# Query projections as products of high and low parts, and work handed between VectorE and GpSimd

## The chip, the cores and the metric

The kernel runs on one core of one Trainium2 chip. The metric is the device time of one execution in microseconds (us), taken as the median of the runs. The chip's engines are TensorE (PE; its weight loads are listed as PEld), VectorE (DVE), ScalarE (ACT), GpSimd (POOL) and SyncE (SP), which issues most of the DMAs. Each has its own queue of instructions and waits for the others on semaphores. SBUF is the memory on the core, PSUM holds the results of TensorE in eight banks of 128 x 512 float32.

## What is computed

The reference, cut to what matters. x has 2 x 1024 tokens of 256 features, the context 2 x 77 rows.

```python
def xattn(q, kv, Wq, Wkv, Wc):                     # q is layernorm(x), kv the context
    qp = jnp.einsum('bld,ed->ble', q, Wq)
    scores = jnp.einsum('bld,bmd->blm', qp, kv)
    idx = jnp.argmax(scores, axis=-1)              # one context row for each token
    mem = jnp.take_along_axis(kv, idx[..., None], axis=1)
    mk, mv = jnp.split(jnp.einsum('bld,ed->ble', mem, Wkv), 2, axis=-1)
    qh = qp.reshape(b, l, 16, 16).transpose(0, 2, 1, 3)
    attn = softmax(jnp.einsum('bhlm...') * 0.25)   # 16 heads, one key and value head
    out = jnp.einsum('bhlm,bmd->bhld', attn, mv)
    return jnp.einsum('bld,ed->ble', out, Wc)

def ffn(x, w1, w2, router_w):                      # 8 experts of 512, 2 for each token
    probs = softmax(x @ router_w.T)
    topk_w, sel = top_k(probs, 2)
    ...                                            # silu(gate) * up, then w2, weighted sum

x = x + xattn(layernorm(x), ctx, Wq, Wkv, Wc)
x = x + ffn(layernorm(x), w1, w2, router_w)
```

Every product must come out nearly as exact as float32, since the choices (argmax, top 2) hang on it.

## The kernel before, in words

**Stages.** 2048 tokens are 16 tiles of 128 (T), taken in NH = 4 chunks of HT = 4 tiles, 512 tokens each (QW). A first stage does, per chunk u, the moments of the layernorm (VectorE), 1/sqrt of the variance as a power (`rs`, GpSimd) and -mean/sqrt (`nm`, GpSimd), the normalised rows `xn` (`x_normal`, ScalarE), their transposition on TensorE (`turn_x`, line 1306 of the kernel) and the copy of it out of PSUM as `xT` (`turned`, ScalarE, line 607; the trace calls it pT, since it lies in that buffer's space). From `xT` come the scores against the context (`score`, line 1319), which use W_q folded into the context beforehand, and the projection to queries (`project`, line 1332).

**The projection.** `project(u, j)` computes 128 of the 256 query features of a chunk: two float32 matmuls of 128 rows by 512 columns. ScalarE rounds the result to fp32r (`q_high`, line 612) and VectorE subtracts that from PSUM to get the rest (`q_low`, line 810); fp32r is a float32 format of fewer bits, which TensorE takes in one pass. High and low parts lie in `qhl`. The later products all use such pairs: high times high, low times high, high times low.

**Picks.** `picks(u)` on VectorE (lines 786 to 806) finds each token's best context row: `sd` (line 791), four `max`, four `max_index`, the scores for the router `x0` (line 800), a cast of the index to float (line 802) and four comparisons with a constant `iota_n` that give one-hot rows `oh` (line 805). `counts(b)` on TensorE sums these for a batch of two chunks, and `picked`, `replaced` and `spread` on VectorE make from it the masked keys `kb` and values `vc` (line 847) of that batch. `logits(u, k)` on TensorE (line 1365) multiplies queries and keys, and `maxima(u, k)` on VectorE (line 861) takes the largest per head. When the eight of chunk 0 are there, they are turned and cast (`maxima_turned`, `mT`, line 616), and the attention proper begins: `scores_turned`, `exps` (line 623), `sums`, `normalise`, `combine`, `residual`, then the router's choice and the placing of tokens into blocks (`choose`, `scaled`, `slots`, `columns`, `hots`, `table`, lines 904 to 990).

**The experts.** From about 140 us on 39 blocks of 128 places are gathered, multiplied with the weights of their expert (`inner`, line 1633, `outer`, line 1642) and added into the output, in a fixed round of TensorE, ScalarE, VectorE and GpSimd.

**The weights' low parts.** The experts' weights (48 pieces of 128 x 512) are loaded as float32 into `raw`. `W` lies over `raw`, two pieces lower. ScalarE's `high` (line 602) rounds a piece to fp32r into `W`, GpSimd's `splits` (line 502) subtracts in two halves of 256 columns and writes the low part as bf16 into a ring of LR = 3 buffers, and SP's `keep_lows` (line 389) stores it to memory, to be read back later. `high` of piece n waits for the low part n - 2, `splits` of piece n >= 3 for the store of n - 3. How many pieces ScalarE takes at which point of its queue is a table, `HIGH_HEAD` for the first stage (seven pieces) and `HIGH_SLOT` for the attention; `exps` stands in the same queue.

**Order.** There is no scheduler: each engine's queue is the order in which its function is written (`@block.tensor` and so on, at the end of each). In the first stage TensorE goes: turns(0), score(0), turns(1), score(1), project(0), router product, counts(0), project(1), turns(2), score(2), project(2), turns(3), logits(0, 0), half of score(3), logits(0, 1), the other half, logits(0, 2), project(3, 0), logits(0, 3), project(3, 1), the other logits. VectorE goes: moments of all chunks, some clearing (lines 1006 to 1013), picks(0), picks(1), q_lows(0), the masks of batch 0, q_lows(1), picks(2), q_lows(2), then maxima with picks(3) and the last q_low between them.

**Buffers with nine elements.** `slot`, `sloti`, `bki`, `rmi` and `rmf` hold 8 numbers and a spare one; `odd()` gives them as 3 x 3.

## Time and profile before

| what | value |
|---|---|
| median of 3 runs | 353.85 us (352.81 to 359.24) |
| the profiled execution | 353.84 us |
| its span, first to last instruction | 352.0 us |
| TensorE, weight loads | 323.9 us (92%), 221.7 us (63%) |
| VectorE, ScalarE, GpSimd | 192.2 (55%), 211.8 (60%), 193.1 us (55%) |
| mean granted clock of TensorE | 0.986 of full speed |
| moved by DMA | 43.77 MB, 124 GB/s |

The profile is of one execution, and its span leaves out 1.84 us around the instructions. A busy time is the sum of the instructions of an engine; TensorE's matmuls are pipelined, so it can be called busy in a stretch in which it isn't at its peak. A float32 matmul is recorded as two. A number behind "x" is a count, L with a number the line of the kernel.

### The profile page before, as it was taken

The numbers are of one execution on the slowest core, as the hardware profiler recorded it, in microseconds if no ns is written. First come the engines' busy times: TensorE is split into PE (matmuls) and PEld (weight loads), VectorE is DVE, ScalarE is ACT, GpSimd is POOL, SyncE is SP. The second block draws the span as 40 slices with busy tenths as digits, with TensorE's granted clock in tenths as the row PEclk, the third lists the DMA queues.
The fourth block names the chain that finished last, engine by engine and source line by source line (L and its number), as shares of the span: only waits on it lengthen the run. The fifth ranks groups of instructions, "written<-read, shape, count | busy, mean of one in ns | idle before, by whom it ended". The sixth has DMA issues, their size and how long they took to land.

```text
span 352.0 us, 7569 instructions
## 1 busy us (share of the span) xinstructions
PE 323.9 (92%) x2324; PEld 221.7 (63%) x2325; DVE 192.2 (55%) x648; ACT 211.8 (60%) x380; POOL 193.1 (55%) x215
## 2 busy tenths in 40 slices
PE   7998989998988899999999999999999999999940
PEld 3855544454444545786767777777777777777730
DVE  3996865636769799787884333333333333333310
ACT  1927427876788693856655556666556665566620
POOL 3401637876868783656766555545555554555330
PEclk9999999999999999999999999999999999999995
DMA  8999535825254377925234432333332333333221
GB/s 239 373 386 387 189 108 163 242 78 181 76 164 151 124 226 242 299 64 153 47 92 64 73 63 49 59 52 53 61 59 34 58 61 61 61 48 51 39 30 15
DMA packets 35690, 43.77 MB, mean 124 GB/s; under 512 B 3312, under 2 KB 28272, under 8 KB 35664
## 3 DMA queue, kind: packets, MB, share of 16 engines
q1 hardware_dynamic: 27088, 32.58, 27.9%
q0 software_dynamic: 7488, 10.39, 18.3%
q10 hardware_dynamic: 1088, 0.46, 0.6%
q8 instruction: 15, 0.25, 0.3%
q14 instruction: 11, 0.09, 0.1%
HBM read 27.49 MB, written 15.93 MB: 123 GB/s over the span
## 4 chain that ended last, share of the span: by engine, by line
PE 67%; POOL 9%; DVE 7%; DMA 6%; issue 6%; ACT 3%; SPq 0%; POOLq 0%; ACTq 0%; DVEq 0%
PE ps L1633 28%; PE ps L1642 15%; POOL low L502 6%; DMA lows<-low 5%; PE ps L1649 5%; PE ps L1332 3%; PE ps L1458 2%; PE ps L1273 2%; PE ps L1618 2%; PE ps L1421 2%; PE ps L1319 2%; POOL ex L535 2%; PE ps L1405 1%; DMA out_x<-xn,idx 1%; ACT pT L623 1%
## 5 line engine op out<-in xcount | busy, mean ns | idle before, releaser
L1633 PE MATMUL ps<-W,kb 128*128 x312 | 95.9, 429 | 0.0
L502 POOL TENSOR_TENSOR low<-raw,W 128x256 bf16<-128x256 f32 x96 | 67.0, 731 | 39.4 <-ACT W L602 31.1
L542 POOL DMA_INDIRECT out_x<-xn,idx x39 | 61.8, 1585 | 46.3 <-ACT xn L721 25.4
L525 POOL DMA_INDIRECT X<-rows,idx x39 | 39.1, 1002 | 47.7 <-ACT xn L721 34.9
L1633 PEld LDWEIGHTS ps<-W,kb 128*128 128x128 f32 x312 | 56.0, 189 | 12.4
L1195 DVE TENSOR_TENSOR kb<-ps,mT 128x512 fp32r<-128x512 f32 x39 | 27.0, 692 | 58.6 <-ACT mT L733 58.5
L1191 DVE TENSOR_TENSOR uT<-uT,ps 128x512 f32<-128x512 f32 x39 | 26.8, 686 | 45.9 <-PE ps L1633 44.3
L1633 PE MATMUL ps<-W1lo,kT 128*128 x156 | 47.2, 384 | 0.0
L721 ACT ACTIVATE xn<-ps,X 128x256 f32<-128x256 f32 x39 | 18.5, 474 | 36.0 <-PE ps L1642 31.7
L711 ACT CAST kb<-ps 128x256 fp32r<-128x256 f32 x39 | 14.5, 373 | 38.0 <-PE ps L1618 34.7
L861 DVE TENSOR_REDUCE mx<-ps 128x8 f32<-128x616 f32 x32 | 25.3, 795 | 20.3 <-PE ps L1365 20.3
L623 ACT ACTIVATE pT<-ps 77x2048 f32<-77x2048 f32 x16 | 29.9, 1871 | 5.1 <-PE ps L1405 5.0
L602 ACT CAST W<-raw 128x512 fp32r<-128x512 f32 x45 | 26.8, 616 | 7.7 <-POOL low L502 7.6
L1642 PE MATMUL ps<-W,mT 128*128 x156 | 28.7, 305 | 1.1 <-ACT mT L733 0.9
L1365 PE MATMUL ps<-kb,qhl 64*128 64x308 f32 x192 | 22.1, 334 | 4.0 <-DVE mx L861 4.0
L735 ACT CAST GT<-mT 128x512 bf16<-128x512 f32 x39 | 24.1, 618 | 1.2
L727 ACT ACTIVATE uT<-ps 128x512 f32<-128x512 f32 x39 | 23.2, 595 | 2.5 <-PE ps L1633 0.2
L1642 PE MATMUL ps<-W,kb 128*128 x156 | 24.4, 279 | 0.0
L1649 PE MATMUL ps<-ident,uT 128*128 128x128 f32 x156 | 23.6, 274 | 0.7 <-DVE uT L1191 0.4
L1642 PE MATMUL ps<-pT,GT 128*128 x156 | 23.8, 275 | 0.0
L1365 PEld LDWEIGHTS ps<-kb,qhl 64*128 64x128 f32 x192 | 14.4, 185 | 14.6 <-issue 12.8
L733 ACT CAST mT<-ps 128x512 fp32r<-128x512 f32 x39 | 22.6, 579 | 1.5 <-PE ps L1649 1.4
(202 smaller groups left out, 529.2 us busy)
## 6 DMA issues: line engine op xcount, KB each, us to landing
raw<-in_w SPq DMA_DIRECT2D x6, 1536.0 KB, 17.4
lows<-low SPq DMA_DIRECT2D x48, 128.0 KB
W1lo<-lows SPq DMA_DIRECT2D x8, 512.0 KB
raw<-in_w SPq DMA_DIRECT2D x6, 512.0 KB, 3.9
rows<-xr SPq DMA_DIRECT2D x4, 528.0 KB
X<-in_x SPq DMA_DIRECT2D x4, 512.0 KB, 7.2
out_x<-X SPq DMA_DIRECT2D x4, 512.0 KB, 3.3
pT<-lows SPq DMA_DIRECT2D x8, 256.0 KB, 4.4
```

Of the source, the lines that this page charges most:

```text
L502: op = pool.tensor_tensor(low[:, n % LR, part], raw[:, n + 2, part], W[:, n, part].bitcast(F32), ALU.subtract)
L525: pool.indirect_dma_start(out=xg[:, b % GR, :], out_offset=None, in_=rows[0:2 * QW, :] if b < EARLY else rows, in_offset=at_rows(b)).then_ ...
L542: pool.indirect_dma_start(out=out[0:2 * QW, :] if c < EARLY else out, out_offset=at_rows(c), in_=ob[:, c % GR, :], in_offset=None, compute ...
L602: act.copy(W[:, n, :], raw[:, n + 2, :]).then_inc(hi_ok, 1)
L623: act.activation(pT[0:NK, 4 * (n % 2):4 * (n % 2) + 4, :], ps[0:NK, 0:4, :], ACT.Exp).then_inc(ex_ok, 1)
L861: dve.tensor_reduce(mx[:, t, u % 2, j * 8:j * 8 + 8].rearrange("p (r h) -> p r h", r=2), ps[:, at:at + 2, 0:HT * NK].rearrange("p r (h n) ...
L1191: dve.tensor_tensor(yb, sg, ps[:, 1, :], ALU.mult).then_inc(y_ok, 1)
L1195: dve.tensor_tensor(y_lo, ps[:, 3, :], y_hi.bitcast(F32), ALU.subtract).then_inc(yl_ok, 1)
L1365: mm = pe.matmul(ps[:, at + r, 0:HT * NK], part[half_, u, j, t * P:(t + 1) * P], kb[half_, u // 2, hl].rearrange("p h n -> p (h n)"), star ...
L1633: mm = pe.matmul(ps[:, f, :], part[:, c * P:(c + 1) * P], chunk(wts, e * WC1 + (2 * c + f)), start=(k == 0 and c == 0), stop=(k == 2 and c ...
L1642: mm = pe.matmul(ps[:, 4, 0:D], part[:, c * P:(c + 1) * P], w2, start=(k == 0 and c == 0), stop=(k == 2 and c == FC - 1))
L1649: mm = pe.transpose(ps[:, 3, c * P:(c + 1) * P], yb[:, c * P:(c + 1) * P], ident[:])
```

## The change

In words:

- All four projections become products of parts. GpSimd casts W_q to fp32r (`wq_hi`) and subtracts (`wq_lo`); ScalarE casts each chunk's `xT` to fp32r (`x_high`), GpSimd subtracts (`x_part(u, 1, c)`). These lie in pieces of `W` that the weights of expert 6 will take. `project_high` does high times high and low W_q times high x, four matmuls; `project_low` high W_q times low x, two. So a chunk has twelve matmuls of fp32r.
- SP waits for all eight of them (`q_mm`, 2 x SPLIT) before the first store of a low part and the loads of experts 6 and 7 behind it.
- On TensorE score(2) stands ahead of project(1), and score(3), whole, ahead of logits(0, 1); on VectorE picks(2) ahead of q_lows(1). `HIGH_HEAD` puts its seven pieces behind q_highs(2).
- `sd` and the clearing of five buffers go from VectorE to GpSimd.
- `iota_n` becomes 7 rows of 11 with a gap of one; the buffers of nine become 8 elements with a gap after each; `lm` and `ex` are stored with the experts outside and the tiles inside, and read the other way.

```diff
-HIGH_HEAD = (0, 0, 2, 3, 2)
+HIGH_HEAD = (2, 2, 3)
...
-        iota_n = sb("iota_n", [P, NK], F16)
+        iota_n = sb("iota_n", [P, NK // RUN, RUN + 1], F16)
...
-        lm = sb("lm", [P, HT, E])
+        lm = sb("lm", [P, E, HT])[:].rearrange("p e t -> p t e")
...
-        sloti = sb("sloti", [P, ODD * ODD], I32)
+        sloti = sb("sloti", [P, 2 * HT, 2], I32)[:, :, 0]
...
+        XS = 2 + 6 * EC
+        wq_hi, wq_lo = W[:, XS, :], W[:, XS + 1, :]
+        def x_part(u, low_part, c):
+            return W[:, XS + 2 + 4 * (u % 2) + 2 * low_part + c, :]
...
+            sp.wait_ge(q_mm, 2 * SPLIT)
             for n in range(E - 6):
...
+            pool.memset(vc[:], 0.0).then_inc(zeroed, 1)
...
+            pool.memset(xr[:], 0.0).then_inc(pad_ok, 1)
             pool.wait_ge(iotas, 12)
             for u in range(NH):
...
+                pool.tensor_tensor(sd[:, here], ve[:, here], rs[:, here], ALU.mult).then_inc(sd_ok, 1)
+                if u == 0:
+                    pool.wait_ge(wqt_in, 16)
+                    pool.tensor_copy(wq_hi, WQT_[:, 0:DC * D]).then_inc(wqh_ok, 1)
+                if u == 1:
+                    pool.wait_ge(wqh_ok, 1)
+                    pool.tensor_tensor(wq_lo, WQT_[:, 0:DC * D], wq_hi.bitcast(F32), ALU.subtract).then_inc(wql_ok, 1)
+
+            for u in range(SPLIT):
+                if u >= 2:
+                    pool.wait_ge(q_mm, 2 * (u - 1))
+                for c in range(DC):
+                    pool.wait_ge(xsh_ok, DC * u + c + 1)
+                    pool.tensor_tensor(x_part(u, 1, c), xT[:, u % 2, c, :], x_part(u, 0, c).bitcast(F32), ALU.subtract
+                                       ).then_inc(xsl_ok, 1)
...
+            def x_high(u):
+                act.wait_ge(xT_ok, 2 * u + 2)
+                if u >= 2:
+                    act.wait_ge(q_mm, 2 * (u - 1))
+                for c in range(DC):
+                    act.copy(x_part(u, 0, c), xT[:, u % 2, c, :]).then_inc(xsh_ok, 1)
...
-                    dve.tensor_scalar(oh[:, u * HT + i, :], iota_n[:], i8f[:, i:i + 1], None, ALU.is_equal
-                                      ).then_inc(oh_ok, 1)
+                    dve.tensor_scalar(oh[:, u * HT + i, :].rearrange("p (a b) -> p a b", b=RUN), iota_n[:, :, 0:RUN],
+                                      i8f[:, i:i + 1], None, ALU.is_equal).then_inc(oh_ok, 1)
...
+            def project_high(u, j):
...
+                for wq in (wq_hi, wq_lo):
+                    for c in range(DC):
+                        pe.wait_ge(xsh_ok, DC * u + c + 1)
+                        pe.matmul(ps[:, 4 + j, :], wq[:, c * D + j * P:c * D + (j + 1) * P], x_part(u, 0, c),
+                                  start=(wq is wq_hi and c == 0), stop=False)
+            def project_low(u, j):
                 for c in range(DC):
-                    mm = pe.matmul(ps[:, 4 + j, :], WQT[:, c, j * P:(j + 1) * P], xT[:, u % 2, c, :],
-                                   start=(c == 0), stop=(c == DC - 1))
+                    pe.wait_ge(xsl_ok, DC * u + c + 1)
+                    mm = pe.matmul(ps[:, 4 + j, :], wq_hi[:, c * D + j * P:c * D + (j + 1) * P], x_part(u, 1, c),
+                                   start=False, stop=(c == DC - 1))
                 mm.then_inc(q_mm, 1)
```

TensorE's queue from score(1) to logits(0, 1), before: L1319 is score, L1332 project, L1514 the router product, L1342 and L1345 counts, L1306 turns, L1365 logits.

```order
L1319 MATMUL ps<-GT,pT 128x85 x8
L1332 MATMUL ps<-pT,WQT 128x512 x4
L1514 MATMUL ps<-RT,uT 128x8 x4
L1342 MATMUL ps<-oh,ones 128x77 x8
L1345 MATMUL ps<-ones,oh 77x1 x8
L1332 MATMUL ps<-pT,WQT 128x512 x4
L1306 MATMUL ps<-ident,xn 128x128 x8
L1319 MATMUL ps<-GT,pT 128x85 x8
L1332 MATMUL ps<-pT,WQT 128x512 x4
L1306 MATMUL ps<-ident,xn 128x128 x8
L1365 MATMUL ps<-kb,qhl 128x308 x6
L1319 MATMUL ps<-GT,pT 128x85 x4
```

The second project (chunk 1) stood ahead of the turns and scores of chunk 2. The same stretch of the changed kernel, from counts on, where L1373 is project_high, L1379 project_low, L1389 and L1392 counts, L1344 turns, L1357 score and L1412 logits:

```order
L1389 MATMUL ps<-oh,ones 128x77 x8
L1392 MATMUL ps<-ones,oh 77x1 x8
L1344 MATMUL ps<-ident,xn 128x128 x8
L1357 MATMUL ps<-GT,pT 128x85 x8
L1373 MATMUL ps<-W 128x512 x4
L1379 MATMUL ps<-W 128x512 x2
L1373 MATMUL ps<-W 128x512 x4
L1379 MATMUL ps<-W 128x512 x2
L1344 MATMUL ps<-ident,xn 128x128 x8
L1412 MATMUL ps<-kb,qhl 128x308 x6
```

Turns and scores of chunk 2 now come first, and a chunk's projection is twelve matmuls where it was four.

GpSimd's queue in the first stage, before: L465 is constants, L485 rs, L487 nm, L502 the low parts of the weights.

```order
L465 IOTA spare 128x1
L465 IOTA iota_n 128x77
L485 TENSOR_TENSOR rs<-ve,half 128x4
L487 TENSOR_TENSOR nm<-ng,rs 128x4
L502 TENSOR_TENSOR low<-raw,W 128x256 x60
```

The pair of rs and nm stood there four times, and the low parts came right behind. The same place in the changed kernel, from the last constant to the low parts (L536), with the repeats of chunks 2 and 3 left out:

```order
L495 MEMSET vc 77x64
...
L499 MEMSET xr 128x1056
L504 TENSOR_TENSOR rs<-ve,half 128x4
L506 TENSOR_TENSOR nm<-ng,rs 128x4
L507 TENSOR_TENSOR sd<-ve,rs 128x4
L510 CAST W<-WQT 128x512
...
L513 TENSOR_TENSOR W<-WQT,W 128x512
...
L520 TENSOR_TENSOR W<-pT,W 128x512 x8
L536 TENSOR_TENSOR low<-raw,W 128x256 x60
```

Clearing, sd, the two operations on W_q and eight subtractions of 512 columns have come in ahead of the first low part.

## Rows read from the trace of the kernel before

**Rows 1.** Page; windows: length, busy PE, PEld, DVE, ACT, POOL, clock, DMA share, GB/s.

```profile
PE 323.9 (92%) x2324; PEld 221.7 (63%) x2325; DVE 192.2 (55%) x648; ACT 211.8 (60%) x380; POOL 193.1 (55%) x215
...
17.50:36.60 19.10, 18.11 (x101) 11.26 (x100) 14.23 (x71) 9.74 (x20) 2.68 (x4) 1.00 1.05 386
36.60:44.70 8.10, 7.22 (x41) 4.04 (x40) 7.88 (x24) 3.45 (x6) 4.99 (x9) 1.00 0.46 157
120.00:136.00 16.00, 15.02 (x153) 7.21 (x141) 14.10 (x62) 14.10 (x19) 10.17 (x16) 1.00 0.76 236
```

**Rows 2.** The chain of waits in order of time: start, length, what.

```profile
17.50 3.47 PE ps L1332 x8
...
27.21 2.02 PE ps L1319 x16
...
46.77 7.20 issue
...
79.39 5.05 DMA lows<-low
```

**Rows 3.** Timeline of VectorE, 36 to 45 us: start, length, what, idle before.

```profile
37.40 0.71 DVE L791 TENSOR_TENSOR sd<-ve,rs 128x4 f32<-128x4 f32 x1
...
40.00 2.19 DVE L805 TENSOR_SCALAR oh<-iota_n,i8f 128x77 bf16<-128x77 f16 x4
42.11 0.79 DVE L861 TENSOR_REDUCE mx<-ps 128x8 f32<-128x616 f32 x1
```

**Rows 4.** Timeline of VectorE, 15 to 27 us.

```profile
15.60 0.94 DVE L1013 MEMSET xr<- 128x1056 f32 x1 [0.17 <-issue]
...
19.00 0.15 DVE L791 TENSOR_TENSOR sd<-ve,rs 128x4 f32<-128x4 f32 x1
...
21.00 0.69 DVE L805 TENSOR_SCALAR oh<-iota_n,i8f 128x77 bf16<-128x77 f16 x4
...
22.88 0.23 DVE L829 SCALAR_TENSOR_TENSOR ps<-ps,desc 128x77 f32<-128x77 f32 x1
...
26.33 1.27 DVE L810 TENSOR_TENSOR qhl<-ps,qhl 128x512 fp32r<-128x512 f32 x2
```

**Rows 5.** The chain of waits again: logits in the attention, products of the experts.

```profile
94.00 0.62 PE ps L1365 x6
...
142.00 2.75 PE ps L1633 x12
```

**Rows 6.** GpSimd: its timeline up to 38 us, and line 496 by itself.

```profile
7.38 1.05 POOL L485 TENSOR_TENSOR rs<-ve,half 128x4 f32<-128x4 f32 x1 [4.91 <-DVE ve L784]
...
16.38 0.20 POOL L487 TENSOR_TENSOR nm<-ng,rs 128x4 f32<-128x4 f32 x1
...
33.92 4.17 POOL L502 TENSOR_TENSOR low<-raw,W 128x256 bf16<-128x256 f32 x6 [17.34 <-ACT W L602]
...
L496 POOL CAST W<-raw x3: 607/616/616, 124.3 to 128.5; 128x512 fp32r<-128x512 f32 x3
```

**Rows 7.** Timeline of ScalarE: two head casts, and the cast of the turned maxima.

```profile
33.22 1.14 ACT L602 CAST W<-raw 128x512 fp32r<-128x512 f32 x2
...
49.70 0.59 ACT L616 CAST mT<-ps 128x512 fp32r<-128x512 f32 x1 [5.27 <-PE ps L1382]
```

**Rows 8.** Timeline of SP's queue: the first stores of low parts.

```profile
35.36 5.61 SPq L389 DMA_DIRECT2D lows<-low  x4
```

**Rows 9.** Lines of VectorE by themselves: duration in ns, least/median/most, first to last start.

```profile
L802 DVE CAST i8f<-i x4: 160/160/198, 18.2 to 39.8; 128x4 f32<-128x4 uint32 x4
...
L847 DVE TENSOR_SCALAR vc<-vv,cc x2: 221/264/308, 25.3 to 64.5; 77x16 f32<-77x16 f32 x2
...
L964 DVE TENSOR_SCALAR rmi<-sloti x4: 154/298/553, 101.1 to 169.8; 128x9 int32<-128x9 int32 x4
...
L969 DVE SCALAR_TENSOR_TENSOR colf<-ef,bki x4: 167/168/583, 102.5 to 170.4; 128x8 f32<-128x8 f32 x4
...
L980 DVE TENSOR_SCALAR oh<-iota_h,colf,tok_f x32: 324/339/350, 105.9 to 175.6; 128x129 f16<-128x129 f16 x32
```

More of the change, by code:

```diff
@@ L29 @@
 HW = HR * HC
-ODD = 3
+RUN = 11
 NK = 77
@@ L187, in build @@
         runs = sb("runs", [P, NH + 1, E], BF16)
[L188 to L189 removed]
+        lm = sb("lm", [P, E, HT])[:].rearrange("p e t -> p t e")
+        ex = sb("ex", [P, E, HT])[:].rearrange("p e t -> p t e")
         base = sb("base", [P, HT, E])
         sme = sb("sme", [P, HT])
[L192 to L196 removed]
+        slot = sb("slot", [P, 2 * HT, 2])[:, :, 0]
+        sloti = sb("sloti", [P, 2 * HT, 2], I32)[:, :, 0]
+        bki = sb("bki", [P, 2 * HT, 2], I32)[:, :, 0]
+        rmi = sb("rmi", [P, 2 * HT, 2], I32)[:, :, 0]
+        rmf = sb("rmf", [P, 2 * HT])
         colf = sb("colf", [P, 2 * HT])
@@ L654, in _ @@
             turns(1)
+            x_high(0)
             x_normal(2)
@@ L658, in _ @@
             act.copy(WC[:, :, D:RW], ps[:, 7, 0:DC * E].rearrange("p (c e) -> p c e", c=DC)).then_inc(wr_out, 1)
+            x_high(1)
+            turns(2)
+            x_high(2)
+            x_normal(3)
+            q_highs(1)
+            turns(3)
+            x_high(3)
+            q_highs(2)
+            high(HIGH_HEAD[0])
+            q_high(3, 0)
             high(HIGH_HEAD[1])
-            q_highs(1)
-            turns(2)
-            x_normal(3)
-            q_highs(2)
+            q_high(3, 1)
             high(HIGH_HEAD[2])
-            turns(3)
-            high(HIGH_HEAD[3])
-            q_highs(3)
-            high(HIGH_HEAD[4])
             maxima_turned(0)
@@ L1024, in _ @@
             spread(0)
+            picks(2)
             q_lows(1)
-            picks(2)
+            maxima(0, 0)
             q_lows(2)
-            maxima(0, 0)
             maxima(0, 1)
@@ L1507, in _ @@
             score(1, range(HT))
-            project(0, 0)
-            project(0, 1)
+            project_high(0, 0)
+            project_high(0, 1)
+            project_low(0, 0)
+            project_low(0, 1)
             pe.wait_ge(rt_ok, 1)
```

84 lines of the change are left out of this document (44 added, 40 removed).

## The prediction

> **What bounds the kernel now.** I read the page first: TensorE is busy 92% of the span, no other engine over 60% [rows 1]. The windows tell where it isn't full: 18.11 of 19.10 us from 17.5 to 36.6, but 7.22 of 8.10 us from there to 44.7, where VectorE is busy 7.88; GpSimd does next to nothing up to 36.6 (2.68 us); the granted clock is 1.00 in all of them, the level of 2.4 GHz [rows 1]. Then the chain of waits: from 17.50 it runs through projections and scores on TensorE, later through the low parts on GpSimd, with 7.20 us of "issue" from 46.77 on [rows 2]. In that hole GpSimd only waits for casts that stand behind the first softmax in ScalarE's queue: the attention lets the low parts start, not the reverse. Last the order of time: VectorE's queue decides when the attention starts. picks(3) takes from 37.40 to 42.11, 4.7 us, and maxima and q_low follow it back to back [rows 3]. The same function took from 19.00 to 21.6, 2.6 us, with GpSimd idle [rows 4]. The change lies ahead of 45 us; what follows, the experts' products from 142 us too, I take as shifted, but for one place at 124 us.
>
> **TensorE's own work.** Projecting a chunk of 512 tokens took 3.47 us for four matmuls (shown as eight) [rows 2]. It becomes twelve of fp32r over 512 columns. Their nearest row is L1633: twelve of 128 rows and 512 columns, eight fp32r and four bf16, in 2.75 us [rows 5], 0.229 each. That is the lower bound (bf16 may be the cheaper third), the old 3.47 the upper one. I take 2.75, the row that it is nearest to: 0.72 us less per chunk, 2.2 for the three chunks ahead of logits(0, 1).
>
> **What is added, and its cover.** (a) W_q is split on GpSimd: a cast of 0.62 us and a subtraction of 512 columns, 1.40 (six of 256 took 4.17) [rows 6]. In its queue they end near 13.7, and TensorE asks at 17.5: hidden; without cover 2.0. (b) Clearing: 0.94 us and five small ones leave VectorE, so picks(0) starts near 15.5 instead of 16.5, where the last of them ended [rows 4]. GpSimd idled 4.91 us ahead of 7.38 [rows 6], so they are hidden there, bounded by 1 and 3 us. (c) Eight casts x_high on ScalarE, 1.14 a pair [rows 7], 4.6 us in all: ScalarE was busy 9.74 of 19.10 us [rows 1]. x_high(0) puts x_normal(2) back by 1.15, but TensorE turns that chunk only near 22: hidden, 1.15 without cover. (d) Eight subtractions on GpSimd, 1.40 each. Those of chunk 0 start when rs, nm and sd of the last chunk are through (16.58 [rows 6] and 0.2 for sd) and end at 19.6; the eight high products end at 17.5 + 1.83 = 19.3: TensorE waits 0.3. Those of chunks 1 to 3 end at least 1 us ahead of their use: hidden. (e) Waits: project_high(u) waits for q_low(u - 1), as before; queued behind it are scores and logits, and VectorE's maxima wait for those. SP waits for all eight projections ahead of its first store of a low part; behind it stand the loads of experts 6 and 7, and GpSimd waits for the stores. Before, they were issued from 35.36 [rows 8].
>
> **The walk without stalls on VectorE.** TensorE came from 17.5 to the end of logits(0, 1) at 36.6. Take off 2.2 for the products and the 1.0 of idle time [rows 1], add the second half of score(3), now ahead of logits(0, 1), 1.0 (a whole one is 2.02 [rows 2]), and 0.4 for waits (0.3 at chunk 0, 0.1 for the turned copy): 34.8. VectorE must have q_low(1, 0) for project(2), which TensorE reaches 2.75 + 2.02 + 0.62 earlier [rows 2, 5], at 29.4: picks(0), picks(1) and q_lows(0) (2.5, 2.5, 1.3 us from 15.5) are through at 21.85, as the counts are, the masks take 3.45 (22.88 to 26.33) [rows 4], picks(2) 2.5, q_low 0.65: 28.45, in time. Then maxima(0, 1) 0.8 and picks(3) 2.5: maxima(0, 2) at 38.1, before 42.11 [rows 3]: 4.0 us gained. About 2.2 of it are picks(3) itself: sd (0.71) is gone, and four comparisons that took 2.19 beside GpSimd's low parts took 0.69 alone [rows 3, 4].
>
> **The walk with stalls.** GpSimd now works from 16.8 to 19.6 and from 21.9 to 27.5, where it did nothing. Beside it VectorE's comparisons took 0.55 instead of 0.17 each and sd 0.71 instead of 0.15 [rows 3, 4]; vc took 0.31 and not 0.22, the index cast 0.20 and not 0.16 [rows 9]. A wait can now be as long as a subtraction of 512 columns. If the cast of picks(0) waits 1.1 and vc 1.2, picks(1) ends at 21.6, and q_lows(0) 1.3, masks 4.65, picks(2) and q_low 3.15 give 30.7; TensorE, held 0.5 at counts(0), waits 0.7 more; maxima(0, 2) come at 39.7 with 0.3 for the cast in picks(3): 2.4 gained. Between 2.4 and 4.0 I take 2.8, nearer to the stalls, since vc and the cast did wait, though little. The rest of the products (2.75 and 0.62 more, then a 0.59 cast: 40.1) is ahead of the last q_low (41.8): hidden.
>
> The comparisons go free by the gap in the constant that they read: L980, built like that (3 rows of 43 into 129), kept 0.32 to 0.35 us wherever GpSimd worked [rows 9]. The page VectorE: DVE Perf Modes in the Trainium skill (What auto-detection actually checks) has a reason: one source runs on two ports if source and destination lie in SBUF and their outermost sizes are both even or equal, which 7 rows of 11 into 77 are not. The trace agrees by L980.
>
> **The late part.** columns(1) lies on the chain at 124 us. rmi took up to 0.55 instead of 0.15, colf 0.58 instead of 0.17 [rows 9], and bki between them is alike: 1.2 us of VectorE if all go free. TensorE was idle 1.0 of the 16 us there [rows 1], and ScalarE only 1.9, so the gain is between 0 and 1.0. I take 0.2: colf has two inputs in SBUF, like sd, which waited, and from 124 us on ScalarE binds nearly as much as VectorE. lm, ex and slot elsewhere are off the chain: 0.
>
> **Sum.** 353.84 (span 352.0 and 1.84 around it) - 2.8 - 0.2 = 350.8. The profiled execution stands on the median, 353.85.
>
> **Rivals.** Rival 1, GpSimd takes it back: a subtraction with fp32r output lasts 2.0 us and not 1.40. For it: GpSimd's rows are rough, and none writes 512 of fp32r from two inputs. Against: a cast of that width took 0.62 [rows 6]. TensorE waits 1.2 more at chunk 0, three stalls grow by 0.6 each, 3.0 in all: 353.6. Rival 2, no stalls, and the late part whole: 353.84 - 4.0 - 1.0 = 348.8. For it: the index cast lost only 0.04. Against: the comparisons lost as long as GpSimd's operation. Rival 3, slower: stores behind the projections. Three head casts stand ahead of mT on ScalarE; each waits for a low part, and that for a landed store. First store at 39.6; low part, cast, low part and cast after it lands make 3.5 us. The longest piece of the chain on a store is 5.05 [rows 2]: mT would come at 48.2, not 46.9, 1.3 of the gain. It decides from a landing of 6.6 us on (mT after 49.70 [rows 7]); with twice the longest, 10.1, mT comes 3.5 late: 357.3. Against: the large loads are over by then. Rival 4, gaps that do nothing in the late part: slot, rmi and bki keep an even count (8), colf, lm and ex keep two inputs in SBUF; all wait as before, so it gives 0: 351.0. For it: rmi waited with equal odd counts (9); against: nothing yet was tried with a gap at a count of 8.
>
> The pages VectorE: DVE Perf Modes (What auto-detection actually checks) and SBUF — State Buffer (SBUF: two separate sides) in the Trainium skill state just rival 4: even sizes on both sides give the two-port mode, and an operation with two SBUF inputs wants the port pair shared with GpSimd anyway, held for the whole instruction. The waits of rmi, colf and sd agree with it.
>
> **Chances.** Forecast 0.42, rival 1 0.15, rival 2 0.15, rival 3 0.05, rival 4 0.23. The forecast's own range is 349.8 to 352.2; the one wanted takes in rivals 1 and 2 with a little scatter, 348.3 to 353.8. 2% of the time, 7.1 us, is about what a measurement of this kernel can tell from no change: faster by more 0.04 (no sum reaches it), slower by more 0.02 (rival 3 with a still later store), within 0.94.
>
> **What would show it.** Twelve fp32r matmuls in 2.7 to 2.8 us; TensorE waiting 0.3 for GpSimd at chunk 0; four comparisons of picks(3) in 0.7; vc or an index cast over 0.5 in the first 30 us; maxima(0, 2) near 39.3 and mT near 46.9, with no wait of ScalarE for low parts; rmi and bki at 0.17 or still at 0.5. I am wrong if TensorE waits over 1 us at a projection, if two of the stalls don't show, or if the gain at 50 us isn't there at 140.

## The result, and the profile after

Over 16 executions of each, before took 354.92 us (median, 352.81 to 359.24) and the changed kernel 352.19 us (350.25 to 357.87). The ratio is 0.9915, 95% interval 0.989 to 0.994: a gain of 3.0 us, which on before's profiled execution of 353.84 makes 350.8, the forecast. It is smaller than 2% of the time, the bound that the prediction had set for a change told from none.

The ratios leave out executions over 1.5% above the fastest of their kernel, so they aren't quite the quotient of the medians; the first profiled execution of the changed kernel was one of those (356.37 us, granted clock 0.970), and the kernel was profiled once more, unchanged (353.85 us, span 351.7, clock 0.979). Rows of "after" are of this second one unless the first is named. It took the same time as before's profiled execution (353.85 and 353.84), so the 3.0 us stand in the medians and not between these two profiles; what the two differ in is read stage by stage below. The page's first line and the three windows answer to [rows 1]:

```profile
PE 321.8 (91%) x2340; PEld 224.7 (64%) x2341; DVE 191.3 (54%) x638; ACT 216.1 (61%) x388; POOL 206.9 (59%) x234
```

Windows: length, busy PE, PEld, DVE, ACT, POOL, granted clock, DMA share, GB/s.

```profile
17.50:36.60 19.10, 17.96 (x124) 14.85 (x122) 15.76 (x68) 12.87 (x25) 11.70 (x12) 1.00 1.02 376
36.60:44.70 8.10, 6.85 (x47) 4.26 (x46) 7.65 (x24) 3.97 (x7) 5.49 (x9) 0.91 0.27 79
120.00:136.00 16.00, 14.93 (x141) 7.21 (x134) 14.35 (x63) 13.19 (x17) 9.75 (x14) 1.00 0.75 234
```

GpSimd went from 2.68 to 11.70 us of the first window, VectorE from 14.23 to 15.76, and the clock of the second is no longer 1.00. VectorE's timeline there answers to [rows 3, 4]. L847 is the index cast, L850 the comparisons, L892 vc, L906 maxima:

```profile
17.05 0.92 DVE L847 CAST i8f<-i 128x4 f32<-128x4 uint32 x1
18.01 0.75 DVE L850 TENSOR_SCALAR oh<-iota_n,i8f 128x77 bf16<-128x77 f16 x4
...
24.97 0.88 DVE L892 TENSOR_SCALAR vc<-vv,cc 77x16 f32<-77x16 f32 x1
...
36.10 0.67 DVE L839 MAX8 m<-ps 128x8 f32<-128x77 f32 x4
...
38.03 0.75 DVE L850 TENSOR_SCALAR oh<-iota_n,i8f 128x77 bf16<-128x77 f16 x4
38.69 0.79 DVE L906 TENSOR_REDUCE mx<-ps 128x8 f32<-128x616 f32 x1
```

The comparisons of picks(3) take 0.75 us for 2.19, the whole of picks(3) 2.59 (36.10 to 38.69) for 4.71, and maxima(0, 2) starts at 38.69 for 42.11. The cast and vc are held up (0.92 for 0.16, 0.88 for 0.22). What held them is GpSimd's queue (answers to [rows 6]; L510 and L513 split W_q, L520 are the x low parts):

```profile
8.76 0.60 POOL L510 CAST W<-WQT 128x512 fp32r<-128x512 f32 x1
...
11.95 1.27 POOL L513 TENSOR_TENSOR W<-WQT,W 128x512 fp32r<-128x512 f32 x1
...
16.65 2.55 POOL L520 TENSOR_TENSOR W<-pT,W 128x512 fp32r<-128x512 f32 x2
21.83 2.50 POOL L520 TENSOR_TENSOR W<-pT,W 128x512 fp32r<-128x512 f32 x2 [2.62 <-ACT W L651]
```

One subtraction takes about 1.26 us. The cast ends at 17.97, when the first one does (16.65 + 1.26 = 17.91). TensorE's timeline answers to [rows 2] (L1373 project_high, L1379 project_low, L1389 counts, L1344 turns, L1412 logits):

```profile
19.26 0.98 PE L1379 MATMUL ps<-W 128*128 128x512 f32 x3 [0.20 <-POOL W L520]
...
21.41 0.47 PE L1389 MATMUL ps<-oh,ones 128*128 128x77 bf16 x8 [0.38 <-DVE oh L850]
...
25.13 1.19 PE L1373 MATMUL ps<-W 128*128 128x512 f32 x4
...
28.00 1.03 PE L1344 MATMUL ps<-ident,xn 128*128 128x128 f32 x8
...
29.98 1.18 PE L1373 MATMUL ps<-W 128*128 128x512 f32 x4 [0.32 <-DVE qhl L855]
```

The chain of waits (start, length, what) now goes through VectorE up to project(2), where [rows 2] had TensorE:

```profile
17.14 0.85 DVE i8f L847
...
25.05 0.80 DVE vc L892
...
29.32 0.61 DVE qhl L855
...
29.98 1.18 PE ps L1373 x4
```

Chunk 1's twelve matmuls take from 25.13 to 28.00, 2.87 us, where four of the old form took 3.53 (22.36 to 25.89 in before's timeline). The turned maxima are cast at 47.80, before at 49.70 [rows 7], and SP's first stores go out at 39.16, before at 35.36 [rows 8]:

```profile
47.80 0.58 ACT L659 CAST mT<-ps 128x512 fp32r<-128x512 f32 x1 [3.31 <-PE ps L1429]
```

```profile
39.16 3.63 SPq L402 DMA_DIRECT2D lows<-low  x4
```

Single lines of VectorE, as in [rows 9]: duration in ns, least/median/most.

```profile
L847 DVE CAST i8f<-i x4: 158/160/923, 17.1 to 37.8; 128x4 f32<-128x4 uint32 x4
L892 DVE TENSOR_SCALAR vc<-vv,cc x2: 345/614/883, 25.0 to 62.6; 77x16 f32<-77x16 f32 x2
L1006 DVE TENSOR_SCALAR rmi<-sloti x4: 152/306/546, 99.3 to 168.6; 128x8 int32<-128x8 int32 x4
L1011 DVE SCALAR_TENSOR_TENSOR colf<-ef,bki x4: 166/168/589, 100.7 to 169.2; 128x8 f32<-128x8 f32 x4
```

rmi still takes 0.55 at its longest and colf 0.59: in the late part nothing has changed.

**The span cut into five.** All kernels can be laid side by side if each profiled span is cut at the start of project(0), of maxima(0, 2), of the first softmax and of the last. The first column is a time, the others are lengths in us:

| kernel | project(0) | to maxima(0, 2) | to first softmax | to last softmax | to the end |
|---|---|---|---|---|---|
| before | 17.33 | 24.78 | 9.44 | 81.44 | 219.0 |
| after, first | 16.41 | 21.97 | 10.99 | 85.68 | 219.2 |
| after, second | 16.73 | 21.96 | 10.97 | 81.54 | 220.5 |

"To maxima(0, 2)" holds the forecast's 2.8 us: 24.78 - 21.96 = 2.82, and 2.81 in the first execution of after. "To first softmax" gives 1.5 of it back, "to last softmax" is unchanged in the second execution and 4.1 longer in the first. So the three columns together show 1.2 us of gain in the second execution and a loss of 3.0 in the first, where the ratio says a gain of 3.0. The start moves by 1.3 us and the last column by 2.4 between executions (all fourteen profiles), so only the three columns between are compared here.

The 1.5 us of "to first softmax" are TensorE's clock. After, in pieces of 2 us:

```profile
40.00:42.00 2.00, 1.01 (x12) 0.53 (x8) 2.00 (x4) 0.28 (x1) 0.97 (x2) 1.00 0.59 197
42.00:44.00 2.00, 1.75 (x13) 1.15 (x14) 1.71 (x4) 0.75 (x2) 2.00 (x4) 0.81 0.21 66
44.00:46.00 2.00, 2.00 (x6) 0.71 (x6) 0.68 (x1) 0.49 (x1) 2.00 (x4) 0.50 0.89 263
46.00:48.00 2.00, 2.00 (x42) 1.45 (x42) 0.80 (x1) 0.20 (x1) 0.58 (x1) 0.83 0.92 222
```

TensorE works half of 40 to 42 us, since logits(0, 5) and logits(0, 6) wait for a maximum (0.6 us each), and from 43.2 to 46.7 the granted clock is 0.50, the level of 1.2 GHz. The four matmuls of constants there take 1.89 us instead of 1.04 (TensorE's timeline, before and after):

```profile
46.98 1.04 PE L1273 MATMUL ps<-tri,ones 128*128 128x512 bf16 x4
```

```profile
43.78 1.89 PE L1311 MATMUL ps<-tri,ones 128*128 128x512 bf16 x4
```

A value like 0.81 is a window in which the level changes: windows that lie wholly inside a stretch show 0.50 or 1.00 here. The Trainium skill, TensorE: Matmul & The Clock Gate (Part 1: The HAM clock gate), has half and full as the two states of this gate; the third level that it names, 13/16, it gives only for three or more busy cores of a die, and this kernel runs on one.

In the first execution the same happened again at 88 us. The waits on TensorE and GpSimd, then two windows:

```profile
87.68 1.94 PE L1468 MATMUL ps<-pT,vc 77*32 77x512 f32 x8 [1.71 <-ACT pT L666]
```

```profile
83.71 4.14 POOL L536 TENSOR_TENSOR low<-raw,W 128x256 bf16<-128x256 f32 x6 [3.19 <-DMA lows<-low]
```

```profile
86.00:88.00 2.00, 0.32 (x4) 0.23 (x8) 1.31 (x6) 2.00 (x3) 1.85 (x3) 0.82 0.38 128
88.00:94.00 6.00, 6.00 (x32) 2.48 (x26) 1.22 (x7) 2.02 (x5) 4.15 (x6) 0.50 0.27 89
```

GpSimd waits 3.19 us for a store of low parts to land (1.92 in the second execution), a weight cast waits for GpSimd, the softmax stands behind that cast in ScalarE's queue, and TensorE waits 1.71 for it (0.46 in the second). Some seven microseconds run at half clock. The wait costs 1.25 us more, the clock most of the rest of the 4.1.

### The profile page after: what moved, and what is told of

Read it like the earlier page. It is cut to its first block, busy times and chain, and to the rows that moved or that the text cites. A ratio compares the mean times of both kernels' runs of the same rounds, so it can differ in the third digit from the quotient of the medians.

```text
span 354.2 us, 7640 instructions
## 1 busy us (share of the span) xinstructions
PE 324.6 (92%) x2340; PEld 225.9 (64%) x2341; DVE 191.6 (54%) x638; ACT 216.2 (61%) x388; POOL 207.0 (58%) x234
## 4 chain that ended last, share of the span: by engine, by line
PE 64%; DVE 16%; DMA 6%; issue 4%; POOL 4%; ACT 3%; ACTq 0%; DVEq 0%; POOLq 0%
PE ps L1687 26%; PE ps L1696 14%; PE ps L1703 4%; PE ps L1412 3%; DMA out_x<-xn,idx 3%; PE ps L1468 3%; PE ps L1505 3%; PE ps L1452 2%; PE ps L1672 2%; DVE mx L906 2%; DMA WKV<-in_WkvT 2%; PE ps L1311 2%; POOL ex L569 2%; POOL low L536 1%; ACT pT L666 1%
## 5 line engine op out<-in xcount | busy, mean ns | idle before, releaser
L536 POOL TENSOR_TENSOR low<-raw,W 128x256 bf16<-128x256 f32 x96 | 67.1, 728 | 21.7 <-ACT W L636 13.4
L906 DVE TENSOR_REDUCE mx<-ps 128x8 f32<-128x616 f32 x32 | 25.4, 796 | 21.7 <-PE ps L1412 21.5
L1412 PE MATMUL ps<-kb,qhl 64*128 64x308 f32 x192 | 22.9, 345 | 3.8 <-DVE mx L906 3.7
L1412 PEld LDWEIGHTS ps<-kb,qhl 64*128 64x128 f32 x192 | 15.1, 193 | 14.3 <-issue 12.4
```

Of the source, the lines that this page charges most:

```text
L536: op = pool.tensor_tensor(low[:, n % LR, part], raw[:, n + 2, part], W[:, n, part].bitcast(F32), ALU.subtract)
L906: dve.tensor_reduce(mx[:, t, u % 2, j * 8:j * 8 + 8].rearrange("p (r h) -> p r h", r=2), ps[:, at:at + 2, 0:HT * NK].rearrange("p r (h n) ...
L1412: mm = pe.matmul(ps[:, at + r, 0:HT * NK], part[half_, u, j, t * P:(t + 1) * P], kb[half_, u // 2, hl].rearrange("p h n -> p (h n)"), star ...
```

## The experiments

Each kernel ran with before on one chip; a ratio is to before's executions there. Eleven edits, and the changed kernel again. All profiles, cut as above:

| kernel | project(0) | to maxima(0, 2) | to first softmax | to last softmax | to the end |
|---|---|---|---|---|---|
| products only | 17.66 | 30.02 | 10.97 | 81.49 | 219.4 |
| handed-over parts only | 17.67 | 22.86 | 10.51 | 84.69 | 219.5 |
| no gap in iota_n | 16.81 | 29.25 | 10.96 | 81.16 | 220.0 |
| the same, TensorE kept busy | 17.76 | 24.25 | 10.79 | 81.10 | 218.7 |
| clearing on VectorE | 16.61 | 25.67 | 10.95 | 81.73 | 219.3 |
| order of before | 16.70 | 23.98 | 9.47 | 81.62 | 221.1 |
| late tiles plain | 17.10 | 21.99 | 9.45 | 81.54 | 220.6 |
| first store free | 17.03 | 21.38 | 9.45 | 82.04 | 220.3 |
| subtractions in halves | 16.84 | 21.31 | 10.94 | 81.87 | 219.5 |
| late gaps filled | 16.53 | 21.77 | 9.47 | 81.65 | 218.9 |
| three edits together | 16.91 | 21.32 | 9.44 | 81.52 | 219.4 |

### The changed kernel again

> The changed kernel once more, unchanged, for a profiled execution at the same granted clock as the one of before and for a ratio of its own. If the gain is the one forecast (2.8 us in the first stage, read from maxima(0,2) near 39 us and mT near 47 us, 0.2 us behind it), the ratio is near 0.9915 and the profiled time is 350.5 to 351.5 us at a granted clock near 0.986. Rival: the early lead of the changed kernel (mT 2.2 us earlier than before's 49.70) is for 0.9 us an earlier start of that one execution, and a drop of the clock gives up part of it, so that a profile at full clock shows mT only 1.3 us earlier; then the ratio lies nearer 0.996.

Ratio 0.9927 (0.9899 to 0.9956), median 352.64 us. maxima(0, 2) came at 38.69 as forecast, mT at 47.80 and not 47, for the clock. Both statements of the expectation have something: the stage gained its 2.8 us, and the clock took 1.5 of it in this execution, so the expected 350.5 to 351.5 us at a clock near 0.986 were not met (353.85 at 0.979). The ratios of the two series are the same within their intervals. The median clock of the executions in this series' ratio is 0.9825 for the changed kernel and 0.9845 for before.

### The products alone

```diff
-        iota_n = sb("iota_n", [P, NK // RUN, RUN + 1], F16)
+        iota_n = sb("iota_n", [P, NK], F16)
...
-            pool.memset(xr[:], 0.0).then_inc(pad_ok, 1)
+            dve.memset(xr[:], 0.0).then_inc(pad_ok, 1)
...
-                pool.tensor_tensor(sd[:, here], ve[:, here], rs[:, here], ALU.mult).then_inc(sd_ok, 1)
+                dve.tensor_tensor(sd[:, here], ve[:, here], rs[:, here], ALU.mult).then_inc(sd_ok, 1)
```

> The four projections as products of high and low parts in their new order, but sd and the clearing are VectorE's again and the comparisons read an unbroken row (no gap in iota_n). Theory of the prediction: the gain of the first stage sits in picks(3) and in the earlier picks(0), that is in VectorE, so TensorE's shorter projections give little alone: picks(3) pays sd 0.71 and about 2.2 instead of 0.7 for its comparisons, maxima(0,2) comes at 41 us or later, the time is 353 to 354 us (ratio 0.998 to 1.001). Rival: TensorE's 0.7 us per chunk projection is what sets the stage; then most of the gain stays (ratio 0.993 or less).

Ratio 1.0124 (1.0065 to 1.0182), 360.77 us. Both expectations fell, and by far: the part of the change that takes work from TensorE makes the kernel slower by 4.4 us when it stands alone. To maxima(0, 2) it needs 30.02 us for 24.78. (One of its six executions took 1764 us, which no row explains; the ratio leaves it out.) TensorE's row of counts:

```profile
25.29 0.70 PE L1390 MATMUL ps<-oh,ones 128*128 128x77 bf16 x8 [3.83 <-DVE oh L846]
```

TensorE waits 3.83 us for VectorE's one-hot rows, and the granted clock is 0.50 from 25.2 to 35.4 us. Further kernels below take that apart.

### The handed-over parts alone

```diff
+            pool.memset(xr[:], 0.0).then_inc(pad_ok, 1)
...
+                pool.tensor_tensor(sd[:, here], ve[:, here], rs[:, here], ALU.mult).then_inc(sd_ok, 1)
...
-                    dve.tensor_scalar(oh[:, u * HT + i, :], iota_n[:], i8f[:, i:i + 1], None, ALU.is_equal
+                    dve.tensor_scalar(oh[:, u * HT + i, :].rearrange("p (a b) -> p a b", b=RUN), iota_n[:, :, 0:RUN],
```

(With the small tiles and the constant itself; before's projections and order stay.)

> The kernel before with three parts of the change alone: clearing on GpSimd, sd on GpSimd, the gap in iota_n; projections and order as before. Theory of the prediction: VectorE no longer sets maxima(0,2), but TensorE's longer projections (3.47 us a chunk) then hand over the last logits of chunk 0 at 42.8 us, so 1.2 to 1.3 us are gained (ratio 0.9965, 352.6 us) and the rest needs the products. Rival: VectorE's load is everything and the products nothing: then the whole gain comes here (ratio 0.992).

Ratio 0.9933 (0.9907 to 0.9959), 353.12 us: 2.4 us of gain where 1.2 to 1.3 were expected (just outside the interval). In the profile VectorE gains 24.78 - 22.86 = 1.9 us to maxima(0, 2), and then 1.07 (10.51 - 9.44) are lost since TensorE hands over the last logits late, as the expectation says:

```profile
42.87 1.11 PE L1369 MATMUL ps<-kb,qhl 64*128 64x308 f32 x12
45.14 1.39 PE L1369 MATMUL ps<-kb,qhl 64*128 64x308 f32 x12 [1.16 <-DVE mx L869]
```

That leaves 0.85 us at the first softmax in this profile, against 2.4 in the ratio. The difference isn't explained; before's own executions lie between 353 and 359 us. This profile had the late store as well (TensorE waits 2.04 us for pT up to 89.69, then 3.4 us run at half clock).

### No gap in iota_n

```diff
-        iota_n = sb("iota_n", [P, NK // RUN, RUN + 1], F16)
+        iota_n = sb("iota_n", [P, NK], F16)
```

(and the comparisons written as in before).

> The changed kernel with an unbroken row in iota_n, nothing else. Theory: the gap is what lets the comparisons run beside GpSimd's subtractions. Without it the four comparisons of picks(3) take about 2.2 us for 0.7, those of picks(0) and picks(1) are stalled beside the chunk subtractions (1.26 us each) too, and maxima(0,2) comes 1.5 us later: ratio to before 0.995 to 0.997. Rival: the comparisons had only been slow by chance of place, or another wait takes the gap's place, and the row's form is worth under 0.3 us: ratio near 0.991.

Ratio 1.0104 (1.0063 to 1.0145), 360.31 us. The mechanism was as expected, the size was not: 1.9% and not 0.4%. VectorE's timeline, then TensorE's:

```profile
18.08 1.68 DVE L850 TENSOR_SCALAR oh<-iota_n,i8f 128x77 bf16<-128x77 f16 x4
...
21.60 2.80 DVE L850 TENSOR_SCALAR oh<-iota_n,i8f 128x77 bf16<-128x77 f16 x4
```

```profile
24.46 0.70 PE L1389 MATMUL ps<-oh,ones 128*128 128x77 bf16 x8 [3.38 <-DVE oh L850]
...
27.26 3.71 PE L1357 MATMUL ps<-GT,pT 128*128 128x85 f32 x16
```

Eight comparisons beside GpSimd's subtractions take 4.48 us instead of 1.50. TensorE has nothing to do for 3.38 us, and after that the scores of chunk 2 last 3.71 us instead of 2.02. The window of 20 to 34 us, for this kernel:

```profile
20.00:34.00 14.00, 10.62 (x59) 9.62 (x58) 11.32 (x52) 6.91 (x14) 4.99 (x4) 0.63 1.05 387
```

The column to maxima(0, 2) grew by 7.29 us. Of it 2.97 are the later counts (7.65 us behind project(0), not 4.68), 3.66 the same work at half clock (counts to the turns of chunk 3: 24.46 to 34.71, in after 21.41 to 28.00), and 1.0 the comparisons of picks(3) (1.75 us); these sum to 7.63, so 0.3 was slack. The counts of the products alone came as late, 7.63 us behind project(0), and their column is only 0.8 us longer than this one: once the gap in iota_n is missing, sd and the clearing on VectorE add only that.

### No gap, but TensorE kept busy

```diff
+            fill(6, 10)
             counts(0)
```

(on the kernel without the gap)

> The changed kernel without the gap in iota_n, and ten matmuls of constants (0.26 us each at the full clock, results read by nobody) on TensorE between the router product and the counts, where that kernel without the gap had TensorE idle for 3.4 us and its granted clock at 0.5 from 22 to 33 us. Theory: of its loss of 1.9 per cent against the changed kernel (6.7 us) only 2.5 to 3 us are the wait itself (counts at 24.46 for 21.41), the rest is the clock that falls after it. With TensorE kept busy the clock stays at 1.00 from 22 to 34 us, and the ratio to before comes to 1.000 to 1.003. Rival: the stalled comparisons cost all of it by themselves, or the clock falls whatever TensorE does: ratio 1.008 or more.

Ratio 1.0033 (1.0003 to 1.0062), 356.32 us. The same kernel without them had 1.0104 and 360.31, so they gain 2.5 us by the ratios and 4.0 by the medians.

```profile
21.42 2.32 PE L1311 MATMUL ps<-tri,ones 128*128 128x512 bf16 x10
23.75 0.47 PE L1389 MATMUL ps<-oh,ones 128*128 128x77 bf16 x8
```

```profile
20.00:34.00 14.00, 13.43 (x96) 10.38 (x95) 13.00 (x57) 9.69 (x20) 6.19 (x5) 1.00 1.05 387
```

The first fence is TensorE's timeline (L1311 the constants, L1389 counts), the second the window of 20 to 34 us. The clock is 1.00 throughout, and the column comes to 24.25: 2.3 us over after, 1.3 of it later counts and 1.0 picks(3). Work whose result nobody reads makes the kernel faster: this shows that the clock, and not only the wait, made the loss. (The comparisons of picks(1) took 1.72 us here and 2.80 there, by where GpSimd stood, so the counts came 1.7 us earlier behind project(0), and these 1.7 of the 5.0 us between the two profiles are not the clock's.) The ratio lies at the upper edge of what was expected for a kept clock, 1.000 to 1.003, and far from the rival's 1.008.

### The clearing back on VectorE

```diff
-            pool.memset(xr[:], 0.0).then_inc(pad_ok, 1)
+            dve.memset(xr[:], 0.0).then_inc(pad_ok, 1)
```

(with the four small tiles; nothing else)

> The changed kernel with the clearing of the five tiles on VectorE again (1.0 us ahead of picks(0)), nothing else. Theory: picks(0) and the counts come 1.0 to 1.6 us later, TensorE's gap ahead of the counts grows from 0.4 us to about 1.5, and as nothing later takes it back maxima(0,2) comes 1.0 to 1.6 us later: ratio 0.995 to 0.997 if the granted clock stays at 1.00 from 20 to 34 us. If a gap of 1.5 us is enough to bring the clock down there (one of 3.4 us was), ratio 1.000 to 1.010. Rival: VectorE has slack behind picks(1), the 1.0 us is taken back before picks(3): ratio 0.990 to 0.993.

Ratio 0.9987 (0.9955 to 1.0019), 354.90 us: 0.6% over the changed kernel's 0.9927, and between the 0.995 to 0.997 expected at full clock and the 1.000 expected as the least with a fall.

```profile
22.53 0.47 PE L1389 MATMUL ps<-oh,ones 128*128 128x77 bf16 x8 [1.65 <-DVE oh L845]
```

```profile
20.00:34.00 14.00, 12.35 (x77) 10.92 (x76) 11.04 (x56) 8.65 (x18) 5.01 (x4) 0.76 1.05 387
```

These are TensorE's row of counts and the window of 20 to 34 us: the smallest cause with a large effect. One microsecond on VectorE brings TensorE's gap from 0.38 to 1.65 us; the counts come 1.2 us later, and the same stretch behind them takes 9.41 us instead of 6.59 (22.53 to 31.94), for the clock. The column grows by 3.7 us. The ratio says 2.1 us more than the changed kernel's; the two need not agree, since one profile is one draw of the clock (its mean was 0.971 here, the lowest of twelve executions that reach to 0.981).

### The order of before

```diff
             counts(0)
-            turns(2)
-            score(2, range(HT))
             project_high(1, 0)
...
             project_low(1, 1)
+            turns(2)
+            score(2, range(HT))
...
-            picks(2)
             q_lows(1)
+            picks(2)
```

> The changed kernel with the order of before: project(1) ahead of the turns and scores of chunk 2 on TensorE, the low parts of q of chunk 1 ahead of picks(2) on VectorE. Theory: project(1) then waits at 22 us for GpSimd's low parts of chunk 1 (first one ready near 23.5 us in the changed kernel), so TensorE idles 0.5 to 1.5 us more and scores(2) and picks(2) come 2.5 us later; VectorE fills that with chunk 1's q, so maxima(0,2) comes 0 to 1 us later: ratio 0.992 to 0.996. If the wait and the one before it together bring the clock down, as in the kernel without the gap, it is 1.00 or more. Rival: the order is worth nothing, ratio 0.990 to 0.993.

Ratio 0.9964 (0.9936 to 0.9992), 353.93 us. TensorE waits 0.72 us for the low parts of chunk 1 at 24.05, and then 0.97 for the rows of chunk 3, which ScalarE normalises behind the late x_high(2). The column to maxima(0, 2) is 2.0 us longer, more than the 0 to 1 expected; the clock kept 1.00. So the new order is worth some 1.3 to 1.7 us by the ratios (0.9964 against the changed kernel's 0.9927 and 0.9915; the intervals overlap) and 2.0 in the column, as a companion of the products: without it they wait for GpSimd. The prediction had not priced it. Two more moves of the change, score(3) as a whole and maxima(0, 0) ahead of q_lows(2) on VectorE, stayed as in the changed kernel and are not priced.

### The late tiles plain

```diff
-        lm = sb("lm", [P, E, HT])[:].rearrange("p e t -> p t e")
+        lm = sb("lm", [P, HT, E])[:]
...
-        rmi = sb("rmi", [P, 2 * HT, 2], I32)[:, :, 0]
+        rmi = sb("rmi", [P, 2 * HT], I32)[:]
```

> The changed kernel with the late part's tiles as before (lm and ex plain, slot, sloti, bki and rmi unstrided). Forecast's rival 4 (strides do nothing in the late part): rmi, bki and colf keep 0.55, 0.52 and 0.58 us at their longest, the time is that of the changed kernel, ratio 0.9915 to 0.993. The forecast's own 0.2 us from the late part: ratio 0.0006 higher. Upper end (1.0 us from the strides): ratio 0.003 higher, near 0.995.

Ratio 0.9905 (0.9873 to 0.9937), 352.45 us. rmi at its longest 0.54 (0.55 with the gaps), colf 0.59 both ways, first to last softmax 81.54 both ways: the gaps do nothing. With the experts outside, lm even costs 0.02 us more each time (median 0.210 for 0.188); the line first in this kernel, then in the changed one:

```profile
L970 DVE TENSOR_TENSOR lm<-g,v x4: 179/188/741, 92.7 to 165.6; 128x32 f32<-128x32 f32 x4
```

```profile
L970 DVE TENSOR_TENSOR lm<-g,v x4: 203/210/769, 93.8 to 166.0; 128x32 f32<-128x32 f32 x4
```

### The first store free

```diff
-            sp.wait_ge(q_mm, 2 * SPLIT)
             for n in range(E - 6):
...
+                    if n == 0 and k == 0:
+                        sp.wait_ge(q_mm, 2 * SPLIT)
                     load(6 + n, 2 * k, 2)
```

(All four first stores now go ahead of the wait; only the loads stay behind it.)

> The changed kernel with the wait for the projections' last matmul taken from ahead of the first four stores of low parts to behind the first of them, so that the first store of the queue does not wait for chunk 3's projection. It tests rival 3 (stores held back behind the projections make it slower): in the changed kernel GpSimd waits 1.45 us for a store at 40.7 us and ScalarE 2.2 us for GpSimd at 42.2 us. Theory: nothing of the path to mT hangs on these, so ratio as the changed kernel, 0.9905 to 0.993. Rival: the later store traffic sets the low parts' pace up to 85 us (the executions that lose 2 us near 86 us do so behind such a store); with the stores earlier the ratio is under 0.990 and the wait near 86 us is gone.

Ratio 0.9900 (0.9864 to 0.9937), 352.33 us. The stores went out at 35.34 and not 39.16, and ahead of mT ScalarE's longest wait for a low part fell from 2.21 to 0.76 us. Nothing came of it, since mT waits for TensorE: 1.81 us at full clock with the late stores (the kernel with the late tiles plain), 3.31 at full clock here. The changed kernel's 3.31 holds the 1.5 us of its clock drop. Near 86 us TensorE still waited 0.81. So rival 3 is ruled out at its place, the stores ahead of mT; a late store near 86 us did cost one execution of after 4.1 us, and this edit leaves that open.

### Subtractions in halves

```diff
-                    pool.tensor_tensor(x_part(u, 1, c), xT[:, u % 2, c, :], x_part(u, 0, c).bitcast(F32), ALU.subtract
-                                       ).then_inc(xsl_ok, 1)
+                    for h in range(2):
+                        part = slice(h * 2 * P, (h + 1) * 2 * P)
+                        op = pool.tensor_tensor(x_part(u, 1, c)[:, part], xT[:, u % 2, c, part],
+                                                x_part(u, 0, c)[:, part].bitcast(F32), ALU.subtract)
+                    op.then_inc(xsl_ok, 1)
```

> The changed kernel with each GpSimd subtraction of the x low parts (512 columns, 1.26 us) cut into two of 256. Theory: the index cast of picks(0) (0.92 us, 0.16 without a stall) and vc (0.89, 0.22 without) are held up to the end of the GpSimd instruction that runs beside them; with halves they lose at most about 0.6 us each, so counts(0) comes 0.2 to 0.5 us earlier, and the time 0 to 0.5 us (ratio 0.990 to 0.992). Rival: the halves cost GpSimd more (each over 0.7 us), TensorE waits longer for the low parts of chunk 0: counts not earlier, ratio 0.993.

Ratio 0.9879 (0.9835 to 0.9923), 351.90 us. The waits are cut as expected (VectorE's timeline; L850 is the cast in this kernel, L895 vc):

```profile
17.16 0.36 DVE L850 CAST i8f<-i 128x4 f32<-128x4 uint32 x1
...
24.54 0.48 DVE L895 TENSOR_SCALAR vc<-vv,cc 77x16 f32<-77x16 f32 x1
```

0.36 for 0.92 and 0.48 for 0.88; GpSimd pays 2.82 for 2.55 us a chunk (0.73 for each half), and TensorE waits 0.47 for the low parts of chunk 0. The column is 21.31, the shortest, but the kernel with the free store has 21.38 by chance of its early phases. The gain is not told from none.

### The late gaps filled, and all three together

```diff
                 for k in range(4, SLOTS):
+                    if k == 5:
+                        pe.wait_ge(sc_used, NH)
+                    if k in (5, 6):
+                        fill(3, 2)
                     logits(0, k)
```

> The changed kernel with two matmuls of constants ahead of each of the logits(0,5) and logits(0,6), in the two gaps of 0.6 us in which TensorE waits for a maximum (40.3 to 42.2 us). Theory: those gaps are what is followed by the granted clock at 0.5 from 43 to 47 us in both profiles of the changed kernel; filled, the clock stays at 1.00 there, mT comes 0.8 to 1.5 us earlier, and the ratio to before is 0.988 to 0.990. Rival: before had the same three gaps of 0.3 to 0.6 us at a full clock, so they are not what sets it: the drop stays, ratio as the changed kernel (0.991 to 0.993).

> The changed kernel with three edits together: subtractions of the x low parts in halves, two matmuls of constants in each of the two gaps ahead of logits(0,5) and logits(0,6), and the late tiles plain again. Theory: the halves give 0.4 us at picks(0) to maxima(0,2), the matmuls of constants keep the clock at 1.00 from 43 to 47 us (1.2 us), the plain tiles take 0.02 us off some twenty instructions that are hidden: 350 us, ratio 0.986 to 0.988. Rival: what sets the end of the first stage does not add up, or the drop near 86 us returns as often: ratio as with the matmuls of constants alone, 0.988 to 0.990.

With the gaps filled the ratio is 0.9884 (0.9846 to 0.9921), 351.03 us, and the clock stays at 1.00:

```profile
42.00:44.00 2.00, 1.98 (x16) 1.05 (x15) 1.84 (x3) 1.15 (x2) 2.00 (x4) 1.00 0.28 83
44.00:46.00 2.00, 2.00 (x41) 1.43 (x42) 0.88 (x2) 0.19 (x2) 2.00 (x4) 1.00 1.00 331
```

All three edits together give 0.9895 (0.9851 to 0.9938), 350.85 us, the lowest median of all; expected were 0.986 to 0.988, and its rival, 0.988 to 0.990, is nearer. Neither is told from the changed kernel's 0.9915. Nor is it shown that the filling keeps the clock: of the ten profiles with the split products and unfilled gaps seven had the drop at this place and three had not (late tiles plain, first store free, order of before); of the five of them taken on the chip of the filled kernels only two had it. Before and the kernel with the old products had none over gaps as long. What the drop costs is certain: maxima(0, 2) to the first softmax is 9.44 to 9.47 us in the six profiles at full clock, and 10.94 to 10.99 in six with the drop (10.79 in one; the fourteenth, the handed-over parts alone, has its 10.51 from the wait shown there).

## Why the prediction was right, and what it left out

**TensorE's work.** 2.75 us a chunk, measured 2.87 with the issue between them, old form 3.53: 0.66 less for 0.72. Right.

**GpSimd.** Subtraction 1.26 for 1.40, the cast 0.60 for 0.62, W_q ready at 13.2 for 13.7, TensorE waiting 0.20 for 0.3 at chunk 0. Right, and rival 1 (2.0 us each) wrong; its sum was a slip too, since 350.8 and 3.0 make 353.8 and not 353.6.

**Stalls.** The cast of picks(0) waited 0.76 (forecast 1.1), vc 0.66 (1.2), the cast in picks(3) nothing (0.3). Both named stalls show, shorter by the shorter subtraction and by where they fell. TensorE waits 0.32 for q_low at project(2), forecast up to 0.7. Rival 2 wrong.

**The comparisons.** 0.75 us for four in all chunks, in chunks 0 and 3 beside GpSimd (in 1 and 2 GpSimd stood idle): right, and the kernel without the gap shows it by taking it away. Alone the unbroken row took 0.69, so the gap itself costs 0.06. The rule of the Trainium skill that was quoted (VectorE: DVE Perf Modes, What auto-detection actually checks) is borne out in both directions: odd rows of 11 into 77 are free, the unbroken row waits, 8 elements wait with a gap as without one (0.55 and 0.54).

**The walk.** 2.8 forecast to maxima(0, 2), measured 2.82 and 2.81 from project(0) on. As a clock time 39.3 was forecast and 38.69 measured, as this execution started 0.6 earlier. Of the 2.82, 2.12 lie inside picks(3) (4.71 us before, 2.59 now; the prediction said about 2.2), and only 0.70 ahead of it. The walk had counted its way there on TensorE, with 2.2 taken off for the products; the chain of waits shows VectorE in that place up to 29.98, so of the three projections only chunk 2's stands on it. mT was forecast near 46.9 and came at 47.80, for the clock.

**The late part.** 0.2 forecast, 0 measured (81.44 before, 81.54 after); rival 4's mechanism was the true one. A term that was too large by its whole size, 0.2 us.

**ScalarE's wait.** "No wait of ScalarE for low parts" was wrong: it waited 2.21 us. It cost nothing.

**What it left out.** The prediction read "the granted clock is 1.00 in all of them" as a property of the kernel. It is one that the kernel keeps only while TensorE's waits are short. Every step that was called hidden, and every price "without cover", was worked out at the full clock: clearing 1.0, stalled comparisons 1.5 in picks(3). Without their cover they cost 3.7 and 7.3 us to maxima(0, 2) in the profiles, because TensorE then has a gap of 1.65 or 3.38 us ahead of the counts and runs seven and ten microseconds at 1.2 GHz behind it. For the same two reasons, the wait and the clock behind it, the parts do not add up: the handed-over parts alone gain 2.4 us, the products alone lose 4.4, both together gain 3.0. So the sum was right in a place where it happened to hold, TensorE's gap ahead of the counts at 0.38 us. A forecast with the true risk would have had a rival "VectorE's stalls open a gap on TensorE and the clock falls", worth 2 to 7 us (2.1 by the ratio with the clearing back, 6.3 without the gap in iota_n, both against 0.9927), and more than 0.02 for slower.

**Luck in the total.** The stage's 2.8 us are shown. That the whole came out at 3.0 is in part luck: the 1.5 us that the clock took back behind that stage in both profiles of after stand in no term of the sum, the late part's 0.2 wasn't there, and no row shows what made up for them in the medians. Of the prediction's own signs of being wrong, the third, a gain at 50 us that isn't there at 140, came up in the first execution: its first softmax is 2.2 us ahead of before's and its last 2.1 behind. In the second both are ahead, by 1.9 and 1.8.

Rival 3's price was wrong for another reason as well: it looked for the danger in SP's queue behind 40 us, where slack was 1.8 us at full clock and 3.3 with the drop, and not in VectorE's at 15 to 21 us, where there is none. After's chain of waits runs through VectorE without a break from 8.31 to 29.93 us.

Still open: why the handed-over kernel gained 2.4 us by its ratio and 0.85 in its profile, hence how much the products add at all (0.9927 against 0.9933 in the same series); where the 3.0 us of the medians lie beyond the 1.2 that the three columns of the second profile show; and what decides whether the clock falls at 43 us.
